# Transposed x and slot embeddings loaded instead of transposed on TensorE, in an attention and soft-MoE kernel

## Time and profile before

| | us |
|---|---|
| median of 3 runs | 820.48 (820.48 to 820.56) |
| the profiled execution | 820.67 |
| its span | 818.9 |
| TensorE busy | 811.9 (99% of the span) |
| VectorE busy | 697.0 (85%) |
| ScalarE busy | 632.6 (77%) |
| GpSimd busy | 169.2 (21%) |

### The profile page before, as it was taken

One profiled execution on the slowest core, in us unless ns is written; L12 is line 12 of the kernel. 1 busy time (PEld: TensorE's weight loads), 2 busy tenths in 40 slices (PEclk: granted clock), 3 DMA queues, 4 the chain that ended last, 5 costly groups with the idle time before them and its releaser, 6 DMA issues.

```text
span 818.9 us, 16705 instructions
## 1 busy us (share of the span) xinstructions
PE 811.9 (99%) x5262; PEld 726.8 (89%) x5262; DVE 697.0 (85%) x1367; ACT 632.6 (77%) x1274; POOL 169.2 (21%) x219
## 2 busy tenths in 40 slices
PE   9999999999999999999999999999999999999997
PEld 8988999888888888887998999999999999999997
DVE  8788988799899989988958888888888889487776
ACT  5666767567787886789668888989888888777775
POOL 0300000043223323542420414141413132000000
PEclk9999999999999999999999999999999999999999
DMA  6111121102323253225102011020202020376893
GB/s 206 68 52 53 52 79 50 53 26 79 109 97 114 92 205 104 78 80 180 50 1 89 16 58 47 26 76 4 98 0 102 0 102 0 102 243 208 274 297 109
DMA packets 52563, 75.38 MB, mean 92 GB/s; under 512 B 3104, under 2 KB 33696, under 8 KB 52384
## 3 DMA queue, kind: packets, MB, share of 16 engines
q1 hardware_dynamic: 52512, 74.76, 27.2%
HBM read 49.59 MB, written 25.17 MB: 91 GB/s over the span
## 4 chain that ended last, share of the span: by engine, by line
PE 96%; DVE 2%; ACT 1%; issue 1%; DMA 0%; DVEq 0%; ACTq 0%
PE bank L1150 22%; PE bank L1194 17%; PE bank L1259 11%; PE bank L1013 10%; PE bank L1038 10%; PE bank L1022 3%; PE bank L880 3%; PE bank L930 3%; PE bank L1142 3%; PE bank L823 2%; PE bank L903 2%; PE bank L891 2%; PE bank L913 2%; PE bank L845 1%; PE bank L856 1%; PE bank L921 1%
## 5 line engine op out<-in xcount | busy, mean ns | idle before, releaser
L1150 PEld LDWEIGHTS bank<-w_r,act_r 128*128 128x128 f32 x1536 | 199.6, 191 | 10.9 <-issue 1.2
L1150 PE MATMUL bank<-w_r,act_r 128*128 128x256 f32 x1536 | 203.2, 282 | 0.0
L1038 PE MATMUL bank<-disp_r,y_r 128*128 128x512 f32 x384 | 103.4, 406 | 0.4 <-DVE disp_r L2262 0.3
L1013 PE MATMUL bank<-yT_r,snT 128*128 128x512 f32 x384 | 99.5, 395 | 0.0
L2474 DVE TENSOR_TENSOR act_r<-act,act_r 128x512 fp32r<-128x512 f32 x112 | 83.6, 753 | 18.2 <-ACT act_r L1701 18.2
L1259 PE MATMUL bank<-eo_r,comb_r 128*128 128x258 f32 x768 | 92.1, 282 | 0.0
L1259 PEld LDWEIGHTS bank<-eo_r,comb_r 128*128 128x128 f32 x768 | 92.0, 189 | 0.0
L1194 PE MATMUL bank<-snT,w_op 128*128 128x512 f32 x336 | 87.2, 394 | 0.2 <-DVE act L2468 0.2
L1013 PEld LDWEIGHTS bank<-yT_r,snT 128*128 128x128 f32 x384 | 71.7, 188 | 16.0 <-issue 0.5
L1038 PEld LDWEIGHTS bank<-disp_r,y_r 128*128 128x128 f32 x384 | 67.7, 189 | 12.9 <-DVE disp_r L2262 0.9
L1701 ACT ACTIVATE act_r<-act 128x512 fp32r<-128x512 f32 x112 | 71.1, 634 | 10.1
(11 more groups left out here) (235 smaller groups left out, 1656.7 us busy)
## 6 DMA issues: line engine op xcount, KB each, us to landing
combine_scratch<-comb SPq DMA_DIRECT2D x64, 256.0 KB, 2.0
stage<-in_w SPq DMA_DIRECT2D x16, 1024.0 KB, 5.4
stage<-combine_scratch SPq DMA_DIRECT2D x4, 2048.0 KB, 9.5
snT<-combine_scratch SPq DMA_DIRECT2D x4, 2048.0 KB, 9.4
x_scratch<-stage SPq DMA_DIRECT2D x8, 512.0 KB, 3.2
x<-x_scratch SPq DMA_DIRECT2D x8, 512.0 KB, 3.9
x_d<-x_scratch SPq DMA_DIRECT2D x8, 512.0 KB, 9.7
slots_eo<-in_x SPq DMA_DIRECT2D x7, 512.0 KB, 4.6
```

What stands on the lines that cost most here:

```text
L1013: last = pe.matmul(bank[m % 2][:, :], snT[:, i, k, m * S:(m + 1) * S], yT_r[:, j, k, :], start=(n == 0), stop=(n == len(steps) - 1))
L1038: last = pe.matmul(bank[4 + k][:, :], y_r[:, i, t, k * P:(k + 1) * P], disp_r[h][:, j, t, :], start=(n == 0), stop=(n == len(fill_steps) - 1))
L1150: done = pe.matmul(bank[BH + 2 * f + c // 2][:, (c % 2) * D:(c % 2 + 1) * D], act_r[:, tile, a, c * S:(c + 1) * S], w2_r[:, w, j, :], star ...
```

## The change

x is loaded a second time in transposed form (made on the host side, like the other weights' layouts), as are the slot embeddings. So TensorE transposes neither. Queries are computed from raw x instead of normalised x: the query weights are centred over the features (a column sum on TensorE, `centre_query_weights` on VectorE), which takes the mean out; the missing 1/std is a factor of the query that cancels in dots / |dots|, except in the floor of the norm, which becomes a value per token (`norm_floor`, `keep_floor`). The sums of xn over the tokens, before a by-product of rounding transposed xn, are now two more columns of ones in the Gram product, whose two row halves go to two banks; ScalarE copies them out (`keep_xsum`). The slot embeddings are no longer scaled before the logits; the logits are scaled by a column of factors when kept. The query's halves are split in TensorE's order: first half, gk, second half, then the value sums; ScalarE keeps the second half after rounding gk. The low part of transposed x is made by VectorE for batch 0 and by GpSimd for batches 1 to 7. SP loads transposed x two batches ahead into two buffers.

```diff
@@ SP @@
             sp.dma_start(wqkvT[:, :, D:3 * D], wqkv_v[:, :, D:3 * D]).then_inc(wkv_loaded, 16)
+            sp.dma_start(xT[:, 0], xt_v[:, 0:KD, :]).then_inc(xT_loaded[0], 16)
             for c in range(2):
                 sp.wait_ge(first_loaded[c], 16)
             load_x(1)
+            sp.dma_start(xT[:, 1], xt_v[:, KD:2 * KD, :]).then_inc(xT_loaded[1], 16)
...
             sp.dma_start(se, slots_in.rearrange("e s d -> s e d")).then_inc(se_loaded, 16)
+            sp.dma_start(seT, slots_t.rearrange("(k p) n -> p k n", p=P)).then_inc(se_loaded, 16)
...
-            with sp.Fori(4, B) as b:
-                sp.wait_ge(x_loaded, 16 * (b - 1))
+            def load_xT(b, u):
+                sp.wait_ge(xT_split, b - 1)
                 alone(sp)
-                store_x2(b - 4)
-                load_x(b)
+                sp.dma_start(xT[:, u], xt_v[:, ds(b * KD, KD), :]).then_inc(xT_loaded[u], 16)
+            load_xT(2, 0)
+            load_xT(3, 1)
+            with sp.Fori(2, PAIRS) as it:
+                for u in range(2):
+                    b = 2 * it + u
+                    sp.wait_ge(x_loaded, 16 * (b - 1))
+                    alone(sp)
+                    store_x2(b - 4)
+                    load_x(b)
+                    load_xT(b, u)
@@ GpSimd @@
+            def rest_of_xT(b, u):
+                pool.wait_ge(xT_hi, b + 1)
+                alone(pool)
+                nc.gpsimd.tensor_tensor(xT_r[:, 1], xT[:, u], xT_r[:, 0].bitcast(F32), ALU.subtract)\
+                    .then_inc(xT_split, 1)
+            rest_of_xT(1, 1)
...
-            pool.wait_ge(se_step, 4)
-            for h in range(HALVES):
...
+            with pool.Fori(1, PAIRS) as it:
+                for u in range(2):
+                    rest_of_xT(2 * it + u, u)
@@ TensorE @@
-            def transpose_xn(b, first, odd=False, it=0):
...
-            def half_of_xn(b):
...
+                    pe.wait_ge(qT_ready, b * KD)
                     pe.wait_ge(xn_split, b + 1)
...
-                    steps = [(t, 0, rhs) for t in range(NT) for rhs in (xn_half[:, t, :], xn_r[:, 1, t, :])]
+                    steps = [(t, i, rhs) for t in range(NT) for i, rhs in ((0, xn_half[:, t, :]), (1, xn_r[:, 0, t, :]))]
                 else:
-                    steps = [(t, i, xn_r[:, j, t, :]) for t in range(NT) for i, j in PASSES]
+                    steps = [(t, i, xn_r[:, j, t, 0:D if j else DZ]) for t in range(NT) for i, j in PASSES]
...
-                queries(b)
-                if odd:
+                queries(b, odd, it, [0])
+                gram_times_k(b)
+                queries(b, odd, it, [1])
+                if odd or not back:
                     value_sums(b)
-                gram_times_k(b)
                 if back:
                     transpose_o(b - 1)
-                if not back:
-                    value_sums(b)
-                    half_of_xn(1)
-                elif not before_y:
-                    transpose_xn(b + 1, False, not odd, it)
...
+            pe.wait_ge(wq_loaded, 16)
+            for k in range(KD):
+                last = pe.matmul(bank[7][:, 0:D], ones_f[:], wqkvT[:, k, 0:D], start=(k == 0), stop=(k == KD - 1))
+            last.then_inc(wq_summed, 1)
...
-            transpose_slots(0)
             attention(2, False, second_back=True)
-            transpose_slots(1)
@@ ScalarE @@
-                sc.wait_ge(se_loaded, 16)
+                sc.wait_ge(se_loaded, 32)
...
-            def round_xnT(b, odd, it=0):
...
+            def round_xT(b, odd):
+                u = int(odd)
+                sc.wait_ge(xT_loaded[u], 16 * (b // 2 + 1))
                 if not is_batch(b, 0):
                     sc.wait_ge(qT_in_psum, b * KD)
+                act_fn(xT_r[:, 0], xT[:, u], ACT.Copy).then_inc(xT_hi, 1)
...
                 if front and not back:
                     sc.wait_ge(wkv_loaded, 16)
                     act_fn(wqkv_r[:, 0, :, D:3 * D], wqkvT[:, :, D:3 * D], ACT.Copy).then_inc(wqkv_hi, 1)
+                    sc.wait_ge(wq_centred, 1)
+                    act_fn(wqkv_r[:, 0, :, 0:D], wqkvT[:, :, 0:D], ACT.Copy).then_inc(wqkv_hi, 1)
+                    round_xT(0, False)
...
                 if front:
+                    keep_xsum(b, odd, it)
                     round_gram(b, not back)
...
-                if front:
-                    keep_qT(b, 1, not back)
...
                 if front:
                     round_gk(b, not back)
+                if front:
+                    keep_qT(b, 1, not back)
                 if front and not back:
                     round_second()
...
                 if following and back:
                     round_xn(b + 1)
-                    round_xnT(b + 1, not odd, it)
+                    round_xT(b + 1, not odd)
@@ VectorE @@
+            def centre_query_weights():
+                dve.wait_ge(wq_summed, 1)
+                v.scalar_tensor_tensor(out=wqkvT[:, :, 0:D], in0=bank[7][:, 0:D].unsqueeze(1).to_broadcast([P, KD, D]),
+                                       scalar=-1.0 / D, in1=wqkvT[:, :, 0:D], op0=ALU.mult, op1=ALU.add)\
+                    .then_inc(wq_centred, 1)
+            def keep_floor(b):
+                v.tensor_scalar(norm_floor[:, ds(b * NT, NT)], mv[:, :, 1], LN_EPS, NORM_EPS * NORM_EPS,
+                                ALU.add, ALU.mult).then_inc(x_mean_kept, 1)
...
-                if is_batch(b, 0) or is_batch(b, 1):
-                    rest_of_xnT(b)
                 if front and not back:
                     rest_of_wqkv(1)
+                    rest_of_wqkv(0)
+                    rest_of_xT(0, False)
                     rest_of_gram(0)
...
                 if following and back:
                     rest_of_xn(b + 1)
-                    rest_of_xnT(b + 1)
...
-                v.tensor_scalar(neg_logits(b, m), bank[m % 2][:, :], -1.0, None, ALU.mult, ALU.min,
+                v.tensor_scalar(neg_logits(b, m), bank[m % 2][:, :], se_scale[:, m:m + 1], None, ALU.mult, ALU.min,
                                 accum_out=dispatch_cols(b, m)[0]).then_inc(logits_kept, 1)
```

More of the change, by code:

```diff
@@ L213, in attention_then_soft_moe @@
         se_loaded = sem("se_loaded")
+        xT_loaded = [sem(f"xT_loaded{u}") for u in range(2)]
         wq_loaded = sem("wq_loaded")
@@ L822, in gram_of_x @@
                             pe.wait_ge(xn_split, 1)
-                        last = pe.matmul(bank[2][:, m * D:(m + 1) * D], xn_r[:, i, t, m * P:(m + 1) * P],
-                                         rhs, start=(n == 0), stop=(n == len(steps) - 1))
+                        last = pe.matmul(gram_bank(b, m)[:, 0:rhs.shape[-1]], xn_r[:, i, t, m * P:(m + 1) * P],
+                                         rhs, start=(n == 0), stop=(n == len(steps) - 1), skip_group_check=True)
                 last.then_inc(gram_in_psum, 1)
@@ L870, in value_sums, with queries @@
                 last.then_inc(sums_in_psum, 1)
-            def queries(b):
-                pe.wait_ge(xnT_split, b + 1)
-                pe.wait_ge(wqkv_split, 1)
+            def queries(b, odd, it, parts):
+                pe.wait_ge(xT_split, b + 1)
+                pe.wait_ge(wqkv_split, 2)
                 if is_batch(b, 1):
                     pe.wait_ge(vb_kept, 1)
+                elif not odd and not is_batch(b, 0):
+                    pe.wait_ge(vb_kept, sums_through(b - 1, True, it))
+                if symmetric(b):
+                    pe.wait_ge(gram_kept, b - THIRD + 1)
+                elif not is_batch(b, 0):
+                    pe.wait_ge(gram_split, b + 1)
                 steps = [(k, i, j) for k in range(KD) for i, j in PASSES]
-                for h in range(KD):
+                for h in parts:
                     for n, (k, i, j) in enumerate(steps):
-                        last = pe.matmul(bank[h][:, :], wqkv_r[:, i, k, h * P:(h + 1) * P], xnT_r[:, j, k, :],
+                        last = pe.matmul(bank[h][:, :], wqkv_r[:, i, k, h * P:(h + 1) * P], xT_r[:, j, k, :],
                                          start=(n == 0), stop=(n == len(steps) - 1))
@@ L894, in outputs @@
             def outputs(b, first):
-                if first:
-                    pe.wait_ge(xnT_split, 2)
-                else:
+                if not first:
                     pe.wait_ge(proj_ready, b)
@@ L1352, in keep_gram, with keep_xsum @@
                 sc.wait_ge(gram_split, b)
-                act_fn(gram[:], bank[2][:, :].rearrange("p (k d) -> p k d", k=KD), ACT.Copy).then_inc(gram_kept, 1)
+                for m in range(KD):
+                    last = act_fn(gram[:, m], gram_bank(b, m)[:, 0:DZ], ACT.Copy)
+                last.then_inc(gram_kept, 1)
+            def keep_xsum(b, odd, it):
+                if not is_batch(b, 0) and not is_batch(b, 1):
+                    sc.wait_ge(sums_in_psum, sums_of_slot(b, odd, it))
+                u = int(odd)
+                if symmetric(b):
+                    sc.wait_ge(gram_kept, b - THIRD + 1)
+                    alone(sc)
```

(7 more changed lines are left out.)

173 lines of the change are left out of this document (82 added, 91 removed).

## The result

The changed kernel takes 826.17 us (median of 7 runs, 823.85 to 828.44) where the kernel before takes 820.48 (820.26 to 820.56): 5.7 us slower, ratio 1.0067, 95% interval 1.0057 to 1.0077. I had forecast 820.6 in a range of 817.3 to 823.2, so the forecast was wrong, in size and in sign. One execution of the kernel with a column of -1 further down took 997.44 us at a mean granted clock of 0.75, a slower state that tells nothing of the edit, and is left out of the range given there.

A forecast was written before the change was run, and what follows sets the result against it. TensorE, 96% of the span, was taken as the bound. Start +0.8, pass 1 +0.8, slots in pass 2 -0.8, passes 2 to 6 -0.66, loads 0 gave +0.14: 820.6 us against the median 820.48, range 817.3 to 823.2.

The forecast's parts named there:

- What leaves TensorE: Transposes of x and of the slots, with batch 1's changes of group, gone from TensorE: together 7.7 us.
- the sum of the attention stage: Start +0.8, pass 1 +0.8, slots in pass 2 -0.8, passes 2 to 6 -0.66, loads 0: +0.14 us.
- no collision in pass 1: If GpSimd and VectorE don't collide in pass 1, the third Gram product starts at T+6.14: -0.8 us.
- The start: First queries wait for a longer chain of weights and transposed x; second Gram product at 19.46, not 18.67: +0.8 us.
- Pass 1: GpSimd, starting first, holds up VectorE's low part of x by the shared port, delaying the Gram product: +0.8 us.
- slots in pass 2 -0.8: In pass 2 TensorE no longer transposes the slots, taken as pure gain: -0.8 us.
- "Nothing" for GpSimd in later passes: After pass 1 the half copy (0.95 us) lies between, and GpSimd is the one that waits: no cost.
- The weight stage: After the attention, with its own feed and VectorE's scale by a column in place of -1: nothing.
- The steady pass: Passes 2 to 6: the output chain to the projection takes T+3.0 or T+3.08, turning most gain into waits: -0.66 us.
- Loads: Transposed x and slots add to SP's early queue; slots in at about 21.6, may land at 21.8: 0, bound +1.9 us.
- The rivals: No pass 1 collision, 819.0 (0.18); no waits, 813.7 (0.13); slots' load late, 822.5 (0.21); GpSimd always first, 835 (0.04).
- GpSimd gets the port first in every pass: Rival: GpSimd first at the shared port, about 2.9 us more in each of 5 passes, 835 us; chance 0.04.

The follow-up runs named there:

- The part with x alone: Changed kernel with slot embeddings scaled by GpSimd and transposed by TensorE as before, logits kept by -1: 823.39 us, ratio 1.0037 to the kernel before.
- both experiments: Changed kernel with GpSimd's low parts of batches 2 and 3 after VectorE's slot low parts: 821.07 us; or with all low parts of transposed x on VectorE: 820.82.
- kernel with the clash removed: Changed kernel where GpSimd makes the low part of transposed x of batches 2 and 3 only after VectorE's slot low parts: 821.07 us, ratio 1.001.
- covering the chain: GpSimd's batches 2 and 3 behind the slots (821.07), plus scaled-output transposes moved ahead of the second query half, ScalarE rounding output first: 818.32 us.
- shortening it: GpSimd's batches 2 and 3 behind the slots (821.07), plus second head's low part of scaled output 2 columns wide except for batch 0: 819.02 us.

## Why the prediction was wrong, point by point

- **What leaves TensorE, and the sum of the attention stage: right once nothing collides, in part by luck.** With GpSimd out of the way the last q times K^T K starts 1.5 us earlier than before. The prediction's terms, with its own value for no collision in pass 1, give +0.8-0.8-0.8-0.66 = -1.5. Measured one by one they are +1.0 (start), -0.8 (pass 1), -0.9 (pass 2), -0.8 (pass 3, said -0.2), -0.2 (passes 4 to 6, said -0.4) and +0.3 (pass 7, said 0). The gain of pass 3 is in no step of mine.
- **The start: right in this execution.** First queries at 12.16 (said 12.3), second Gram product at 19.50 (said 19.46). The column sum took TensorE 1.1 us, not under 0.5, but almost all of it lies before the first Gram product would start anyway: 8.04 for 7.90.
- **Pass 1: the mechanism right, the instruction wrong.** VectorE was first by 0.10 us where I had GpSimd first by 0.35: ScalarE began to round the output at T+1.03, not T+0.72, as it waited for TensorE's transposes. So pass 1 gave -0.9 us where the sum has +0.8, which hid part of the miss. The part with x alone shows the collision as I had drawn it, VectorE ending 1.08 us after GpSimd.
- **The step that failed: "slots in pass 2 -0.8", with "Nothing" for GpSimd in later passes.** Passes 2 and 3 came out at +0.1 and +2.3 where I had -0.9 and -0.2. I counted what TensorE no longer does for the slots and never costed what replaces it on VectorE. The transposed slots come from SBUF and no longer from PSUM, so their low part became an instruction with two SBUF inputs, and it stands in VectorE's line right behind the low part of x, where GpSimd is at work in passes 1 and 2. I had asked "what collides with GpSimd?" of one instruction and closed the matter for later passes with "the half copy lies between"; it moves GpSimd away from the low part of x (56.44 and 57.27) and onto the slots' (57.77).
- **What it cost.** The changed kernel's run at a mean clock of 0.999 took 823.85; against 821.07 without the clash that is 2.8 us of waits. The median run, 826.17 at 0.996, is 2.3 above that, and I put this down to half clock: 0.003 of 823 us is some 2.5 us of full clock missing, and a stretch costs 1.5. Together 5.1, which both experiments gave back. The split is an estimate, and the forecast had no term for the clock at all.
- **The weight stage: "nothing" was 2.0.** I had said that it has its own feed, and looked up no price for a column. By experiment 0.8 to 1.05 of it is the column, though VectorE is not the bound there by its busy time. The other 1 us lies in TensorE's groups of logits, about 0.02 us on each, and its cause stays open. The kernel with the clash removed came to 821.07, close to the forecast of 820.6, only because an attention stage 1.6 us better than my sum met this weight stage, 1.9 worse.
- **The steady pass: right from T to the projection.** T+3.02 (even) and T+2.98 (odd), said 3.08 and 3.0. The waits that should show it are smaller than the 0.5 to 0.7 that I named, 0.30 for oT_r in odd passes and 0.18 for gk_r in even ones, and passes 4 to 6 gained 0.1 together, not 0.4. That covering the chain gives 2.75 us, and shortening it 2.05, shows that it is this chain which eats what the transposes free.
- **Loads: right for the slots, not for the start.** ScalarE begins the squares of the slots at 19.98 (said by 21.8), and TensorE shows no wait for slots. But I asked only when the added loads land, not what they do to the key and value weights ahead of them. In four of the ten profiled executions of kernels with transposed x these came about 1 us later or more, and the start with them; in the changed kernel's own they did not. That the added loads cause this is likely, since the kernels without them don't have it, but no experiment shows it.
- **The rivals.** None of them was the case. "GpSimd gets the port first in every pass", with 0.04, had the right mechanism; I had priced it only at the low part of x, and all or nothing. The nearest miss is a rival that I didn't write: the same port with any of VectorE's other two-SBUF instructions.

## What to carry to other kernels

When an engine gets a new instruction that shares something with another engine, list every instruction of the other that can fall beside it, those that the same change alters above all: a source moved from PSUM to SBUF changes what an instruction collides with, not what it computes. When work leaves the bounding engine, the first thing to look for is the chain that its place was covering; reordering so that other work of the bounding engine lies there (here the second query half) is what turns the saving into time. A stall in a full TensorE can be followed by a stretch at half clock, here about 1.5 us in those executions that had it, whatever the length of the stall. So read several executions before putting a number on either.

## What the hardware showed that I had not expected

- One idle time of 0.92 us, in a TensorE that is otherwise full, was followed by 3.4 us at 1.2 GHz; a wait of 2.65 us in another kernel was not, and one of 0.34 us was. So the length of the idle time alone doesn't decide, and most of the spread between runs of the changed kernel goes with their mean clock (823.85 us at 0.999 to 828.44 at 0.993, where the kernel before stays in 0.3 us).
- Who started first, by 0.1 to 0.25 us, decided whether VectorE's low part of x took 1.22 or 3.23 us, and whether GpSimd's took 2.40 or 3.37.
- One and the same load of 512 KB, with the same loads issued around it, took 4.8 to 5.5 us to land in six executions and 6.4 to 7.1 in four.
- A multiplication with running minimum from PSUM takes 743 ns by a column and 684 by a constant, on 128x512.
